# A mixture-of-experts layer on one core: down product of the 64-row sets with the weights stationary

## The reference

```python
probs = jax.nn.sigmoid(logits)
scores, indices = jax.lax.top_k(probs, TOP_K)      # two of eight experts for each token
g = jax.nn.silu(jnp.einsum('th,ehi->tei', xf, gate_w))
u = jnp.einsum('th,ehi->tei', xf, up_w)
combined = jnp.einsum('tei,eih,te->th', g * u, down_w, w)
return shared + combined.reshape(b, s, h)
```

## Time and profile before

| what | value |
|---|---|
| time, median of 3 executions | 554.63 us (553.48 to 555.42) |
| the profiled execution's own time | 559.31 us |
| its span, first to last instruction | 557.6 us |
| mean granted clock of TensorE | 0.99 of full speed |
| PE busy | 512.9 us, 92% of the span |
| ACT, DVE, POOL busy | 55%, 58%, 52% |

### The profile page before, as it was taken

One profiled execution on the slowest core, in us unless ns is written; L12 is line 12 of the kernel. 1 busy time (PEld: TensorE's weight loads), 2 busy tenths in 40 slices (PEclk: granted clock), 3 DMA queues, 4 the chain that ended last, 5 costly groups with the idle time before them and its releaser, 6 DMA issues. The chain is left out here.

```text
span 557.6 us, 14828 instructions
## 1 busy us (share of the span) xinstructions
PE 512.9 (92%) x4757; PEld 424.7 (76%) x4757; DVE 321.5 (58%) x904; ACT 306.7 (55%) x581; POOL 290.8 (52%) x242
## 2 busy tenths in 40 slices
PE   4898988899999999997889899999999999999991
PEld 3466777688888888886667689888897888988880
DVE  4788998789897878878535234323342333233330
ACT  3889896777887675754234344444443443444440
POOL 3547776768786775858022434443533533434444
PEclk9899999999999999999999999999999999999997
DMA  8698857969794947514565765745748547345543
GB/s 270 190 191 179 180 152 127 192 183 199 187 205 134 199 125 160 155 70 135 139 114 79 96 106 69 101 70 74 107 60 88 77 60 92 49 71 78 69 50 38
DMA packets 139350, 68.54 MB, mean 123 GB/s; under 512 B 114608, under 2 KB 132336, under 8 KB 139280
## 3 DMA queue, kind: packets, MB, share of 16 engines
q1 hardware_dynamic: 126128, 48.84, 43.5%
q0 software_dynamic: 13152, 18.76, 19.7%
HBM read 19.46 MB, written 23.08 MB: 76 GB/s over the span
## 5 line engine op out<-in xcount | busy, mean ns | idle before, releaser
L2216 PE MATMUL bank<-xn2t,w 128*128 128x256 f16 x1608 | 184.5, 273 | 3.3 <-issue 2.0
L2216 PEld LDWEIGHTS bank<-xn2t,w 128*128 (+1 forms) x1608 | 155.6, 98 | 24.8 <-issue 2.3
L1661 DVE SCALAR_TENSOR_TENSOR th<-th,bank 128x512 f32<-128x512 f32 x83 | 56.8, 685 | 74.5 <-ACT th L998 68.2
L998 ACT ACTIVATE th<-bank 128x512 f32<-128x512 f32 x83 | 49.4, 596 | 77.3 <-PE bank L2216 62.4
L2240 PE MATMUL bank<-w,h 128*128 (+1 forms) x768 | 91.0, 273 | 0.0
L2240 PEld LDWEIGHTS bank<-w,h 128*128 128x128 f16 x768 | 74.6, 98 | 8.9
L871 POOL DMA_INDIRECT out<-p,wm x28 | 44.5, 1590 | 65.9 <-ACT p L1331 26.6
L1478 DVE TENSOR_TENSOR h<-th,h 128x512 f16<-128x512 f32 (+1 forms) x69 | 49.3, 715 | 40.9 <-ACT h L948 40.0
L948 ACT ACTIVATE h<-th 128x512 f16<-128x512 f32 (+1 forms) x69 | 42.9, 622 | 47.3 <-DVE th L1661 38.7
L739 POOL TENSOR_TENSOR w<-wst,w 128x768 f16<-128x768 f32 x36 | 59.1, 1645 | 16.6 <-ACT w L948 16.2
L763 POOL DMA_INDIRECT rows<-xrow,sidx x56 | 57.9, 1033 | 17.0 <-issue 13.3
(11 more groups left out here) (186 smaller groups left out, 793.0 us busy)
## 6 DMA issues: line engine op xcount, KB each, us to landing
wst<-w_all SPq DMA_DIRECT2D x36, 384.0 KB
x<-x SPq DMA_DIRECT2D x8, 512.0 KB, 6.1
out<-x SPq DMA_DIRECT2D x8, 512.0 KB
rows<-xrow POOLq DMA_DIRECT2D x1, 1192.5 KB, 7.2
rows<-xrow,sidx POOLq DMA_INDIRECT x56
out<-p,wm POOLq DMA_INDIRECT x28
xn2t<-rows SPq DMA_TRANSPOSE x26
wm<-rows SPq DMA_DIRECT2D x26, 9.0 KB, 2.2
```

What stands on the lines that cost most here:

```text
L998: a.activation(th[:, half * 512:(half + 1) * 512], G[half][:, :], *gate_fn(t)).then_inc(f_tanh, 1)
L1661: d.scalar_tensor_tensor(out=tb, in0=tb, scalar=1.0 / WS if by_silu(t) else 0.5 / (WS * WS), in1=U[half][:, :], op0=ALU.mult, op1=ALU.mult ...
L2216: ins = mm(dst, w_ap(j, ws, m * MAT + k * I + (2 * half + i) * P, P), moving(ms * KD + k), start=(cnt == 0), stop=(cnt == 3 * KD - 1))
```

## The change

`half_down` now has the weights as the stationary operand (128 by 128) and streams 64 columns of the activations, 12 products for each of two halves of the 256 output columns. The result stands transposed, output columns in the partitions and rows along the bank, in 128 columns of the bank that the old result did not use. ACT copies it to a float16 high part (`yt_high`), DVE makes the low part (`yt_low`), and PE turns it back with four products by an identity (`half_back`), 128 moving columns each. `half_down` moves ahead of the pair's `down`; `half_back` takes its old place. DVE writes the identity and a strip of zeros once, before group 2, which now stands ahead of the loop on DVE.

```diff
@@ buffers, in space of x1 that is free by then
+        yt = x1[:, 12 * P:14 * P + P].bitcast(F16)
+        ident16 = x1[:, 16 * P:16 * P + P // 2].bitcast(F16)
@@ ACT
+            def yt_high(m):
+                act.wait_ge(yt_mm, m + 1)
+                wait(act, dh_mm, m)
+                copy(yt[:, 0:P], YS[:, D:D + P]).then_inc(yt_hi, 1)
...
-            def ffn_half_and(t, half, *entries):
+            def ffn_half_and(t, half, *entries, back=None):
                 tanh(t, half)
                 for n in entries:
                     expert(n)
+                if back is not None:
+                    yt_high(back)
                 split_h(t, half)
...
-                ffn_half_and(t, 0, 2 * i - 1)
+                ffn_half_and(t, 0, 2 * i - 1, back=m if 0 <= m < HALVES else None)
@@ DVE
+            def yt_low(m):
+                dve.wait_ge(yt_hi, m + 1)
+                low(yt[:, P:2 * P], YS[:, D:D + P], yt[:, 0:P]).then_inc(yt_lo, 1)
...
-                ffn(t, 0)
+                ffn_half(t, 0)
+                if back:
+                    yt_low(i - FIRST_HALF - 1)
+                ffn_low(t, 0)
...
-            with dve.Fori(2, SINGLES - 4) as i:
+            dve.wait_ge(out_done, 16 * B)
+            d.memset(yt[:, 2 * P:2 * P + HP], 0.0).then_inc(id16_rdy, 1)
+            d.tensor_copy(ident16, ident[:, :]).then_inc(id16_rdy, 1)
+            group(FIRST_HALF, back=False)
+            with dve.Fori(FIRST_HALF + 1, SINGLES - 4) as i:
                 group(i)
@@ PE, half_down
                 pe.wait_ge(fh_lo, m + 1)
                 pe.wait_ge(ys_read, singles)
+                wait(pe, yt_lo, m)
+                for a in range(2):
+                    cnt = 0
+                    for i in range(KI):
+                        for ws, hs in PASSES:
+                            ins = mm(YS[:, D + a * HP:D + (a + 1) * HP],
+                                     w_ap(j, ws, 2 * MAT + i * D + a * P, P),
+                                     h_h[:, (hs * KI + i) * HP:(hs * KI + i + 1) * HP], start=(cnt == 0),
+                                     stop=(cnt == 3 * KI - 1))
+                            cnt += 1
+                ins.then_inc(yt_mm, 1)
+            def half_back(m):
+                if m == 0:
+                    pe.wait_ge(id16_rdy, 2)
+                pe.wait_ge(yt_lo, m + 1)
                 wait(pe, yh_read, m)
...
-                        ins = mm(YS[:, 0:D], h_s[:, 1024 + (hs * KI + i) * HP:1024 + (hs * KI + i) * HP + P],
-                                 w_ap(j, ws, 2 * MAT + i * D, D), start=(cnt == 0), stop=(cnt == 3 * KI - 1))
-                        cnt += 1
+                for a in range(2):
+                    for part in range(2):
+                        c = part * P + a * HP
+                        ins = mm(YS[:, a * P:(a + 1) * P], yt[:, c:c + P], ident16, start=(part == 0),
+                                 stop=(part == 1))
                 ins.then_inc(dh_mm, 1)
@@ PE, group
+                if 0 < passed <= HALVES:
+                    half_down(passed - 1, min(i + 3, SINGLES))
                 down(t - 1, expert(2 * i - 1))
                 if 0 < passed <= HALVES:
-                    half_down(passed - 1, min(i + 3, SINGLES))
+                    half_back(passed - 1)
```

More of the change, by code:

```diff
@@ L290, in build @@
         fh_tanh, fh_h, fh_hi, fh_lo = (sem(f"fh_{n}") for n in ("tanh", "h", "hi", "lo"))
+        yt_mm, yt_hi, yt_lo, id16_rdy = (sem(n) for n in ("yt_mm", "yt_hi", "yt_lo", "id16_rdy"))
         y_out = sem("y_out")
@@ L1412, in group @@
             def group(i):
-                t = 2 * i + SHARED
-                ffn_half_and(t, 0, 2 * i - 1)
+                t, m = 2 * i + SHARED, i - FIRST_HALF - 1
+                ffn_half_and(t, 0, 2 * i - 1, back=m if 0 <= m < HALVES else None)
                 y_copy_of(2 * i - 1)
-                if 0 <= i - FIRST_HALF - 1 < HALVES:
-                    y_copy_half(i - FIRST_HALF - 1)
+                if 0 <= m < HALVES:
+                    y_copy_half(m)
                 ffn_half_and(t, 1, *[PAIRS + i + 3] * (i + 3 < SINGLES))
@@ L2129, in half_h, with group @@
                 low(h_h[:, TT:2 * TT], th_h, h_h[:, 0:TT]).then_inc(fh_lo, 1)
-            def group(i, single=True, half=True):
+            def yt_low(m):
+                dve.wait_ge(yt_hi, m + 1)
+                low(yt[:, P:2 * P], YS[:, D:D + P], yt[:, 0:P]).then_inc(yt_lo, 1)
+            def group(i, single=True, half=True, back=True):
                 t = 2 * i + SHARED
-                ffn(t, 0)
+                ffn_half(t, 0)
+                if back:
+                    yt_low(i - FIRST_HALF - 1)
+                ffn_low(t, 0)
                 ffn(t, 1)
@@ L2176, in _ @@
             for i in range(SINGLES - 3, GROUPS - 1):
-                group(i, single=False, half=False)
+                group(i, single=False, half=False, back=i - FIRST_HALF - 1 < HALVES)
             ffn(SHARED + PAIRS - 2, 0)
@@ L2635, in half_down @@
                 pe.wait_ge(ys_read, singles)
-                wait(pe, yh_read, m)
-                cnt = 0
-                for i in range(KI):
-                    for hs, ws in PASSES:
-                        ins = mm(YS[:, 0:D], h_s[:, 1024 + (hs * KI + i) * HP:1024 + (hs * KI + i) * HP + P],
-                                 w_ap(j, ws, 2 * MAT + i * D, D), start=(cnt == 0), stop=(cnt == 3 * KI - 1))
-                        cnt += 1
+                wait(pe, yt_lo, m)
[13 more added lines that the diff above has]
+                pe.wait_ge(yt_lo, m + 1)
+                wait(pe, yh_read, m)
+                for a in range(2):
[3 more added lines that the diff above has]
+                                 stop=(part == 1))
                 ins.then_inc(dh_mm, 1)
```

## The result

The changed kernel takes 559.0 us in the median of 22 executions (555.15 to 562.92), the kernel before, in the same runs, 554.75 us (550.8 to 561.26). The ratio is 1.0081, with a 95% interval of 1.006 to 1.0102: slower by 0.8%, 4.5 us by the ratio. Every ratio in this document leaves out the executions that took over 1.5% longer than the fastest of the same kernel, so it can differ a little from that of the medians (here 1.0077). The forecast was 558.9 us.

What follows compares the result with a forecast made beforehand. PE was taken to bound the kernel. Per half 1.8 + 0.22 - 1.31 = +0.71 us, +5.0 us for seven, less 0.7 us of DMA wait: +4.3 us on 554.63 gives 558.9 us; 80% range 556.5 to 561.0 us.

Steps and rivals of the forecast that it cites:

- What bounds: PE, busy 92% of the span: a microsecond on its list in groups 3 to 9 reaches the end one for one.
- (a): Half's down product: 12 products of 256 columns removed in each of seven groups, 1.31 us per half.
- (b): Added products alone: 0.70 us for the 24 short ones, 0.22 us for the four, 0.92 us per half.
- (c): Register operations of the 24 short products, ahead of the pair's down product: the run costs 1.8 us, not 0.70.
- (d): Group 6, PE's 0.83 us wait for a DMA: 0.7 us given back, or nothing.
- (e): ACT and DVE: the transposed result's high and low parts have 2.2 us of cover; moved copies cost nothing.
- The queue is full enough: Sequencer far enough ahead of the 24 short products: 553.5 us (chance 0.11) or 551.9 us (0.05).
- The weight loads bind: Twice as many weight loads, 98 ns each, one behind another: +10 us, 564.5 us; chance 0.03.
- A new wait that swallows more: Turned-back product waits for its low part, or POOL's additions back up; 1 us would give 566 us; chance 0.04.
- absorption: The vanished DMA wait and other slack take the loss, within 0.3% (under 1.7 us); chance 0.05.

Runs made afterwards that it cites:

- split kernel: Changed kernel, read moved behind the four products, 24 short products cut into 12 ahead of the pair's down product and 12 between its halves; ratio 1.0036.

## Why the prediction was right

*What bounds.* Right as far as the runs tell: 4.3 us were forecast, PE's stretch grew by 4.32 us in the two traces, the ratio says 4.5 us (3.3 to 5.7). That it reaches the end one for one is not shown by the two traces, whose tails differ by 2.5 us. Better evidence are two kernels with tails of 13.0 and 13.1 us: from the one without register operations to the changed one with one more read the stretch grows from 200.31 to 212.25 us, 11.9 us, and the ratio from 0.997 to 1.0136, 9.2 us, each with an interval of about 2 us to either side.

*(a), (b)* 1.31 us less and 0.22 us more, as counted. The products alone would take 0.70 us; both the kernel without register operations and the one with the run behind the down product show just that.

*(c)* The run was put at 1.8 us and took 1.84, so a half cost 0.75 us more and not 0.71, +5.25 us in all for the +5.0 of the sum. The lead decided, as said: 0.4 us gives 1.86 in the group shown, 0.9 gives 1.17, 1.6 gives 0.70, and none at all, with PE standing still first, 2.0 + 0.5.

*(d)* The wait in group 6 did not shrink by 0.7 us but vanished, 1.0 us by the starts. With such waits in the traces of six of the eleven experiments, in other groups too and of 0.2 to 2.9 us in total, this term is luck of one execution: that the forecast of 4.3 us meets the stretch's 4.32 to a few hundredths comes from (c) a little too low and (d) a little too small. The sum would have been as good with any value between 0 and -1.0.

*(e)* The copy took 277 ns (278 said), the low part 293 (287), and it was done at 366.55 us, 2.0 us ahead of the four products (2.2 said). One thing I had missed: the pair's own high part on ACT (`split_h`) did not start 0.4 us later but 1.9: it waits for the first half of the pair's down product, which had moved (367.51 us, 3.4 us after the run's start; 1.6 before). It costs nothing, since its result is needed some 10 us later. 

*The rivals.* "The queue is full enough" is what the kernel with the run behind the down product shows, 0.70 us at a lead of 1.6 us; in the changed kernel's place it did not hold. What decided was the lead of 0.4 us in the changed kernel, which came from what the sequencer had to execute just before. The depth of 64 that the Trainium skill gives for TensorE's queue (TensorE: Matmul & The Clock Gate, "Architectural detail: the array is 16× 32×32, not 1× 128×128") is neither contradicted nor shown by a run here. "The weight loads bind" is refuted by 0.70 us. A new wait that swallows more did not come in the changed kernel, but did in the split one. Of absorption PE's stretch shows none; for the tail it is open.

*What stays open.* Why the tail is 15.5 us in the trace before and 13.1 us in the one after. Why the load of a table read takes 0.30 us mostly and up to three times that in some places. Whether a PE that is ahead by 2.7 us makes the singles' DMAs late more often, or whether this was chance: the kernel without register operations was as short, had no such wait, and its ratio was 0.997. And why ACT's copy in four of the seven groups of the split kernel started up to 0.8 us later than in the other three, where it started at once.

## What to carry to other kernels

Where the sequencer has no lead left, a run of products costs what the sequencer executes for it, if that is more than their streaming time. Before long products are replaced with twice as many short ones, count the register operations, table reads and waits ahead of them, and read in the trace how far ahead of PE the sequencer is at that very place. Short products belong behind long ones, and a table read behind long ones too; an early wait on PE's queue spends the lead even where PE itself would not have waited, and a read directly behind it then decides what that costs: 0.06 us with a load of 0.30 us, over 1 us with one of 0.9 us.

## What the runs showed of the hardware

A register operation on PE's queue is recorded with 32 ns but spaced 0.11 to 0.12 us from the next one. A table read into a register, with what follows it, takes 0.65 to 0.7 us of the sequencer, of which the load is 0.30 us. That is the median: of the 45 to 52 loads in a trace 6 to 16 take over 0.35 us, in the changed kernel up to 0.99 us.

```profile
L2555 PEldq TENSOR_LOAD <-w_tab x45: 295/303/992, 262.3 to 522.7; - x45
```

A wait on PE's queue holds the sequencer: in the split kernel the read behind it started at 374.0 us, 0.1 us after the low part was done (373.92 us), while PE had products to execute until 374.43 us. In a trace a stall of this kind can bear the name "issue", or that of an engine whose result had been there already, or none at all: in the changed kernel PE counts as busy throughout the 1.84 us.
